# Spectral filter's channel mixing: from whole-array products, one unit at a time, to 64-row tiles of TensorE, two units at once

## The chip, the cores and the metric

The kernel runs on one core of a Trainium2 chip. The metric is the device time of one execution in microseconds, median of several runs. In the profile PE is TensorE's matmul, PEld its weight load, DVE is VectorE, ACT ScalarE, POOL GpSimd, and SPq the queue from which most DMAs are issued. All times are microseconds unless marked ns.

## What is computed

Two layers work on x, (2, 128, 128, 128) in fp32: two images of 128 by 128 tokens with 128 channels. Each layer (weights left out of the signature):

```python
def layer(x):
    residual = x
    h = afno_filter(layer_norm(x, n1_g, n1_b), w1, b1, w2, b2)   # + its own input
    h = h + residual
    residual = h
    h = gelu(layer_norm(h, n2_g, n2_b) @ mw1 + mb1)               # 128 -> 512
    return h @ mw2 + mb2 + residual                               # 512 -> 128

def afno_filter(x, w1, b1, w2, b2):                               # channels in 8 blocks of 16
    xf = rfft2(x, axes=(1, 2), norm='ortho')                      # 128 x 65 frequencies
    xr, xi = real(xf), imag(xf)                                   # einsum: block-diagonal 16 x 16
    o1r = relu(xr @ w1[0] - xi @ w1[1] + b1[0])
    o1i = relu(xi @ w1[0] + xr @ w1[1] + b1[1])
    o2r = softshrink(o1r @ w2[0] - o1i @ w2[1] + b2[0], 0.01)
    o2i = softshrink(o1i @ w2[0] + o1r @ w2[1] + b2[1], 0.01)
    return irfft2(o2r + 1j * o2i, s=(H, W), axes=(1, 2), norm='ortho') + x
```

## The kernel before

The program is a list of four steps, two layers by two images (`STEPS`), and in each step PE's queue is written as `dft_w`, `filter_`, `idft_h`, `mlp`. The engines' queues are written out by hand and meet in counting semaphores; nothing reorders them.

`dft_w` transforms along the width: 32 groups of four channels, each a 128x512 PSUM bank, evicted by ACT and DVE (`evict_a`) into the spectra, whose layout is (column frequency, channel half, real or imaginary, 64 channels of the half).

`filter_` is the stage that the change touches. Its work is cut into 34 units (`UNITS`): a unit n is four column frequencies (`GROUP`) of one channel half, q = n % 2; units 0 and 1 hold frequencies 0 to 3, units 2 and 3 ("alone") the Nyquist column only, the rest four frequencies each. Per unit:

- PE `dft_h` (L562): transform along the height, four fp32 products of 128 columns into bank q (0 or 1). A product's 128 output rows are 64 channels real and 64 channels imaginary.
- ACT `g_copy` (L826) copies that bank to `gsb`; for the first two units it also copies the Nyquist rows to `nyq` (L829).
- PE `mix1` (L573): the first complex mixing with the block-diagonal `w1s` as stationary operand, 128 by 128; the even part (L583, 65 of each 128 columns) and the odd part (L585, 63) use different weights. Output in bank 2 + q.
- ACT `e_copy` (L834) copies the even part to `usb`; DVE `combine` (L1089, two instructions, L1095 and L1096) adds and subtracts the odd part from PSUM; ACT `o_relu` (L840) adds the bias and takes the relu into `osb`.
- PE `mix2` (L606): four products with the data `osb` as stationary operand (128 by 128) and `w2s` as the moving one (128 columns), output transposed, in bank 4 + q.
- DVE `shrink` (L1099): bias (L1105, out of PSUM into `vsb`), clamp (L1107), difference (L1120, into the arena for the inverse transform).

The order around it: PE's loop in `filter_` (L616) is mix1 of unit n + 1, dft_h of a later unit (four ahead in the count), mix2 of unit n. `mix1` of a unit waits until `combine` of the unit two before it (the same bank) is done (`u_out`), `mix2` waits for `o_relu` (`o_out`) and for L1105 of the unit two before it (`v_out`). DVE's loop `batch` (L1266) is combine of the next unit, shrink of this one. `edges` mixes frequency 0 and Nyquist together once a step (PE L643, DVE L1122 and `edges_out` L1136). In the first step PE ends the filter with `keep_warm` products, in the later ones with `fc1_held`, the MLP products of a tile held back from the step before. `idft_h` begins when all but the last shrink are done.

The weights are built from packed blocks: DMAs into `wraw`, `vectors`, `b2rep` (on ACT's queue for layer 0, L886 to L893, on SP's for layer 1, `load_spectral` L391), multiplied by masks on POOL (`build_spectral`), scaled on DVE (`scale_spectral`) after a small product on PE (`dc_bias`).

The fences of rows further down name these lines; an fp32 product of the source appears in them as two loads and two matmuls.

## Time and profile before

| | us |
|---|---|
| median of 3 runs (lowest, highest) | 1652.82 (1651.64, 1653.29) |
| the profiled execution, its time | 1653.2 |
| the profiled execution, its span | 1651.4 |
| PE busy in the span | 1598.6 (97%) |
| PEld busy | 1445.4 (88%) |
| DVE busy | 1076.1 (65%) |
| ACT busy | 938.4 (57%) |
| POOL busy | 619.8 (38%) |

The granted TensorE clock is at its full level in all slices of the span. In the page, a group's row gives the line, engine, operation, output and input with their shapes, how many there were, busy time and mean duration. In a timeline a row gives the start, the length of the merged group, engine, line and operation; matmuls are pipelined, so the time that one takes up on PE is the distance of starts and not its own duration. A shape such as 64*128 64x65 is 64 rows by 128 columns of weights, with 65 moving columns.

### The profile page before, as it was taken

Reading aid. Unit: us, or ns where it says so; the run is one execution under the profiler, and the core shown is the slowest. Engines: PE = TensorE matmul, PEld = TensorE weight load, DVE = VectorE, ACT = ScalarE, POOL = GpSimd, SP = SyncE. Lnnn points to the kernel's source line nnn. Section 1 sums busy time; section 2 is a strip of 40 time slices with the busy share of each in tenths; the row PEclk is TensorE's granted clock in tenths of the full one; section 3 lists DMA queues with packets and bytes.
Section 4 is the critical chain, followed back from the end, with each engine's and each line's share of the span. In section 5 each row is a group of like instructions: output and inputs, shape, how many; then the busy total and the mean of one; then the engine's idle time right before and its main releaser. Section 6 shows DMA issues by size and latency. Waiting matters only on the chain.

```text
span 1651.4 us, 34968 instructions
## 1 busy us (share of the span) xinstructions
PE 1598.6 (97%) x11278; PEld 1445.4 (88%) x11278; DVE 1076.1 (65%) x2697; ACT 938.4 (57%) x1782; POOL 619.8 (38%) x774
## 2 busy tenths in 40 slices
PE   0999999999999999999999999999999999999999
PEld 0999988888999988888899998888889998888888
DVE  7889566556559856655656966665664995555453
ACT  5655276666535546666644545666663553666665
POOL 4800046766800016676660002677673000211111
PEclk9999999999999999999999999999999999999999
DMA  7500713333300062333320042333331006011111
GB/s 222 197 15 1 238 45 108 95 102 121 97 14 1 8 236 83 108 95 102 122 78 1 1 166 94 101 108 101 102 110 46 1 1 204 27 32 38 32 39 45
DMA packets 167249, 137.67 MB, mean 83 GB/s; under 512 B 9459, under 2 KB 131189, under 8 KB 167157
## 3 DMA queue, kind: packets, MB, share of 16 engines
q1 hardware_dynamic: 166354, 136.23, 26.1%
q8 instruction: 59, 0.97, 0.3%
q10 hardware_dynamic: 802, 0.21, 0.1%
q14 instruction: 34, 0.27, 0.1%
HBM read 69.29 MB, written 67.11 MB: 83 GB/s over the span
## 4 chain that ended last, share of the span: by engine, by line
PE 79%; DVE 14%; issue 4%; ACT 1%; SPq 1%; DVEq 1%; DMA 1%; POOL 0%; ACTq 0%
PE ps L756 27%; PE ps L558 7%; PE ps L722 7%; PE ps L724 7%; PE ps L683 7%; PE ps L723 7%; DVE vsb L1105 4%; PE ps L716 3%; PE ps L702 3%; PE ps L708 3%; DVE csb L1107 3%; DVE usb L1095 3%; DVE usb L1096 2%; PE ps L568 2%; PE ps L612 2%
## 5 line engine op out<-in xcount | busy, mean ns | idle before, releaser
L756 PEld LDWEIGHTS ps<-mw,gel 128*128 128x128 f32 x4000 | 520.6, 191 | 42.3
L756 PE MATMUL ps<-mw,gel 128*128 128x128 f32 x4000 | 523.7, 274 | 0.0
L875 ACT ACTIVATE gel<-ps,mb1f 128x512 f32<-128x512 f32 x500 | 343.7, 687 | 250.5 <-PE ps L724 219.7
L1460 POOL TENSOR_TENSOR arena<-arena,mb2rep 128x512 f32<-128x512 f32 x125 | 160.1, 1281 | 654.6 <-ACT hn L861 654.6
L722 PE MATMUL ps<-hth,mw1h 128*128 128x512 f32 x512 | 260.3, 508 | 2.9 <-DVE htl L1206 1.5
L1449 POOL TENSOR_SCALAR arena<-xnext,rstd,shift 128x128 f32<-128x128 f32 x360 | 159.3, 462 | 207.6 <-DVE shift L1344 207.6
L861 ACT ACTIVATE hn<-arena,shift,rstd 128x128 f32 (+1 forms) x512 | 221.7, 483 | 16.7 <-DVE shift L1344 16.7
L1189 DVE TENSOR_TENSOR arena<-ps,arena 128x512 f32 (+1 forms) x60 | 41.5, 691 | 252.4 <-PE ps L708 233.8
L724 PE MATMUL ps<-hth,mw1l 128*128 128x512 f32 x512 | 202.1, 395 | 0.0
L723 PE MATMUL ps<-htl,mw1h 128*128 128x512 f32 x512 | 200.8, 392 | 0.0
L846 ACT ACTIVATE osb<-usb,vectors 128x512 f32<-128x512 f32 (+1 forms) x136 | 95.6, 703 | 158.3 <-DVE usb L1096 158.3
L1206 DVE TENSOR_TENSOR htl<-ps,hth 128x512 fp32r<-128x512 f32 x128 | 88.2, 689 | 97.3 <-ACT hth L869 97.3
L612 PE MATMUL ps<-w2s,osb 128*128 128x128 f32 x1040 | 140.4, 277 | 2.3 <-ACT osb L846 2.3
L568 PEld LDWEIGHTS ps<-cst,arena 128*128 128x128 f32 x1024 | 132.9, 191 | 6.5 <-issue 0.8
L568 PE MATMUL ps<-cst,arena 128*128 128x128 f32 x1024 | 135.9, 276 | 0.3
L612 PEld LDWEIGHTS ps<-w2s,osb 128*128 128x128 f32 x1040 | 126.9, 192 | 6.9 <-ACT osb L846 6.3
L1407 POOL TENSOR_TENSOR gz<-arena,gain 128x512 f32<-128x512 f32 x96 | 123.7, 1290 | 7.0
L558 PE MATMUL ps<-cst,arena 128*128 128x128 f32 x1024 | 121.4, 282 | 1.0 <-POOL arena L1420 1.0
L558 PEld LDWEIGHTS ps<-cst,arena 128*128 128x128 f32 x1024 | 120.9, 196 | 1.1 <-DVE arena L1063 1.1
L869 ACT CAST hth<-ps 128x512 fp32r<-128x512 f32 x128 | 75.2, 587 | 80.1 <-PE ps L716 80.1
L683 PEld LDWEIGHTS ps<-cst,arena 128*128 128x128 f32 x1024 | 115.3, 192 | 1.3
L683 PE MATMUL ps<-cst,arena 128*128 128x128 f32 x1024 | 116.1, 275 | 0.0
(118 smaller groups left out, 2397.9 us busy)
## 6 DMA issues: line engine op xcount, KB each, us to landing
arena<-aside SPq DMA_DIRECT2D x128, 256.0 KB, 5.0
aside<-gz SPq DMA_DIRECT2D x96, 256.0 KB, 3.0
between<-xout SPq DMA_DIRECT2D x62, 256.0 KB, 2.3
out_dram<-xout SPq DMA_DIRECT2D x62, 256.0 KB, 2.3
xnext<-between SPq DMA_DIRECT2D x60, 256.0 KB, 3.1
aside<-first SPq DMA_DIRECT2D x32, 256.0 KB, 2.3
xnext<-in_x_dram SPq DMA_DIRECT2D x30, 256.0 KB, 3.1
first<-in_x_dram SPq DMA_DIRECT2D x1, 960.0 KB, 7.2
```

The source lines that it names most:

```text
L558: mm = pe.matmul(ps[:, 2 + cg % 4, P * i:P * i + P], rows_of(s)[:, (GROUP * cg + i) // 2, :, i % 2], FW, start=True, stop=True)
L568: mm = pe.matmul(ps[:, q, P * i:P * i + P], spec_of(s)[:, GROUP * b + i, q].rearrange("p r c -> p (r c)"), FH, start=True, stop=True)
L612: mm = pe.matmul(ps[:, 4 + q, P * i:P * i + P], osb[:, q, i, :], w2s[:, q].rearrange("p r c -> p (r c)"), start=True, stop=True)
L683: mm = pe.matmul(ps[:, cg % 4, P * i:P * i + P], y_of(s)[:, q, ch, :], IH, start=True, stop=True)
L722: pe.matmul(bank, h, hth[:, r % 2, :], start=True, stop=False)
L723: pe.matmul(bank, h, htl[:, r % 2, :], start=False, stop=False)
L724: pe.matmul(bank, l, hth[:, r % 2, :], start=False, stop=True).then_inc(f1_mm, 1)
L756: mm = pe.matmul(ps[:, r % 2, P * i:P * i + P], gel[:, r % 2, m, P * i:P * i + P], mw2[:, s // IMAGES, m, :], start=(m == 0 and i == 0), s ...
L861: ins = act.activation(hn[:, r % 2, i, :], row, ACT.Identity, bias=shift[:, r // 2, r % 2 * ROWS + i:r % 2 * ROWS + i + 1], scale=rstd[:, ...
L875: act.activation(gel[:, r % 2, m, :], ps[:, 2 + m % 2], ACT.Gelu, bias=mb1f[:, s // IMAGES, m:m + 1]).then_inc(gelu_out, 1)
L1449: ins = pool.tensor_scalar(zrow(s + 1, h0 + k), pairs(xnext[:, r, k, :]), rstd[:, r // 2, row:row + 1], shift[:, r // 2, row:row + 1], ALU ...
L1460: pool.tensor_tensor(t, t, b, ALU.add).then_inc(mb2_done, 1)
```

## The change

The channels of each half q are laid out anew in the spectra. Before, the 128 rows of a unit were (64 real, 64 imaginary); after, they are (g, real or imaginary, 32 channels), with g a half of the channel half. As the mixing is block-diagonal in blocks of 16 channels, no product crosses g, so a 128 by 128 weight matrix becomes two of 64 by 64, on rows 0 to 63 and 64 to 127. For q = 1 the two g change places between rows of the input and rows of the output.

- `mix1` now takes a pair p of units (n = 2p and 2p + 1) and issues, for the even and the odd part, four products of 64 rows and 64 output rows: (q, g) on rows 64 g, output rows 64 (g ^ q). It waits for both `gsb` copies and for `combine` of both units of the pair before; the semaphore rises by two at the last product.
- `mix2` takes the pair as well: for q, frequency and g a product with 64 rows of `osb` (128 columns) as stationary operand and 64 columns of `w2s`, output in banks 4 to 7, alternating by pair; again one rise at the end.
- PE's order is mix1 of pair p + 1, mix2 of pair p, both dft_h of pair p + 2. DVE's is combine of a unit of the next pair, shrink of a unit of this pair, for q = 0, 1. ACT's is both e_copy, o_relu, both g_copy, o_relu.
- The Nyquist unit reads `gsb` directly (32 rows deep), so `nyq` and its copies are gone.
- `edges` comes after mix2 of pair 4, and pair 5 waits for `edges_out`; `keep_warm` and `fc1_held` move behind the last mix2.
- `w1s`, `w2s` and the masks are half as wide; the blocks are loaded in 13 pieces with `b2rep` (`load_weights`), and the vectors in five (`load_vectors`), on SP's queue behind the constants in layer 0. The loops over evictions of the spectra are split in two by g.

The diff, cut to its core:

```diff
-            def mix1(s, n):
-                g, q = spectrum_of(n), n % 2
-                alone = n in (2, 3)
+            def mix1(s, p):
+                alone = p == 1
                 if not alone:
-                    pe.wait_ge(g_out, 2 * BATCHES * s + g + 1)
-                if n >= 2:
-                    pe.wait_ge(u_out, UNITS * s + n - 1)
...
+                    pe.wait_ge(g_out, 2 * BATCHES * s + spectrum_of(2 * p + 1) + 1)
+                if p:
+                    pe.wait_ge(u_out, UNITS * s + 2 * p)
+                def quarters(j0, j1, depth, k0, k1, kind, start):
+                    for q in range(2):
+                        for g in range(2):
+                            own_rows = slice(HALF * g + depth[0], HALF * g + depth[1])
+                            cols = slice(HALF * (g ^ q), HALF * (g ^ q) + HALF)
...
+                            mm = pe.matmul(dst[:, :, k0:k1], w1s[own_rows, kind, q].rearrange("p r c -> p (r c)"),
+                                           gsb[own_rows, q, j0:j1, k0:k1], start=start, stop=True, skip_group_check=True)
+                    return mm
...
+                elif p:
+                    quarters(0, GROUP, (0, HALF), 0, EVEN, 0, True)
+                    mm = quarters(0, GROUP, (0, HALF), EVEN, P, 1, False)
...
-                mm.then_inc(m1_mm, 1)
+                mm.then_inc(m1_mm, 2)
-            def mix2(s, n):
-                q, kws = n % 2, 1 if n in (2, 3) else GROUP
-                pe.wait_ge(o_out, UNITS * s + n + 1)
-                if n >= 2:
-                    pe.wait_ge(v_out, UNITS * s + n - 1)
-                for i in range(kws):
-                    mm = pe.matmul(ps[:, 4 + q, P * i:P * i + P], osb[:, q, i, :],
-                                   w2s[:, q].rearrange("p r c -> p (r c)"), start=True, stop=True)
-                mm.then_inc(m2_mm, 1)
+            def mix2(s, p):
+                kws = 1 if p == 1 else GROUP
+                if p >= 2:
+                    pe.wait_ge(v_out, UNITS * s + 2 * p - 2)
+                for q in range(2):
+                    pe.wait_ge(o_out, UNITS * s + 2 * p + q + 1)
+                    for i in range(kws):
+                        for g in range(2):
+                            own_rows = slice(HALF * g, HALF * (g + 1))
+                            at_ = 2 * HALF * 2 * q + HALF * i
+                            mm = pe.matmul(ps[:, 4 + 2 * (p % 2) + g, at_:at_ + HALF], osb[own_rows, q, i, :],
+                                           w2s[own_rows, q].rearrange("p r c -> p (r c)"), start=True, stop=True)
+                mm.then_inc(m2_mm, 2)
...
+                for p in range(PAIRED):
+                    if p + 1 < PAIRED:
+                        mix1(s, p + 1)
+                    if p == EDGE_PAIR + 1:
+                        pe.wait_ge(y_done, (UNITS + 1) * s + 2 * EDGE_PAIR + 2)
+                    mix2(s, p)
+                    if p == EDGE_PAIR:
                         edges(s)
+                    if p and p + 2 < PAIRED:
+                        for q in range(2):
+                            dft_h(s, 2 * p + 4 + q)
+                if s:
+                    fc1_held(s, 0)
+                    fc1_held(s, 1)
+                else:
+                    pe.wait_ge(v_out, UNITS * s + UNITS - 2)
+                    keep_warm(8, 6)
...
-                    g_copy(s, n + 1, 1)
-                    e_copy(s, n, 0)
+                    for q in range(2):
+                        e_copy(s, n + q, q)
                     o_relu(s, n, 0)
                     if not last:
-                        g_copy(s, n + 2, 0)
-                    e_copy(s, n + 1, 1)
+                        for q in range(2):
+                            g_copy(s, n + 2 + q, q)
                     o_relu(s, n + 1, 1)
...
+                def batch(b, odd, last=False):
                     for q in range(2):
-                        if not (last and q):
-                            combine(s, 2 * b + 3 + q, 1 - q)
-                        shrink(s, 2 * b + 2 + q, b, q)
...
+                        if not last:
+                            combine(s, 2 * b + 4 + q, q)
+                        shrink(s, 2 * b + 2 + q, b, q, odd)
```

## Rows read from the trace of the kernel before

**Rows 1.** The page: span, and busy time of the engines.

```profile
span 1651.4 us, 34968 instructions
...
PE 1598.6 (97%) x11278; PEld 1445.4 (88%) x11278; DVE 1076.1 (65%) x2697; ACT 938.4 (57%) x1782; POOL 619.8 (38%) x774
```

**Rows 2.** The page: chain that ended last, its shares by engine.

```profile
PE 79%; DVE 14%; issue 4%; ACT 1%; SPq 1%; DVEq 1%; DMA 1%; POOL 0%; ACTq 0%
```

**Rows 3.** Busy time in a window of the filter of step 1, with its header.

```profile
core 0: us, PE busy (x) PEld busy (x) DVE busy (x) ACT busy (x) POOL busy (x), PEclk, DMA share, GB/s
520.00:552.00 32.00, 32.00 (x243) 30.66 (x241) 29.76 (x61) 17.91 (x37) 0.00 (x0) 1.00 0.00 1
```

**Rows 4.** Timeline, one unit (start, length, engine, line, operation, shapes).

```profile
519.76 0.60 PE L583 MATMUL ps<-gsb,w1s 128*128 128x260 f32 x2
519.96 0.69 DVE L1105 TENSOR_TENSOR vsb<-ps,b2cols 128x512 f32<-128x512 f32 x1
...
520.20 0.59 PE L585 MATMUL ps<-gsb,w1s 128*128 128x252 f32 x2
...
520.62 1.05 PE L568 MATMUL ps<-cst,arena 128*128 128x128 f32 x8
...
521.51 1.06 PE L612 MATMUL ps<-w2s,osb 128*128 128x128 f32 x8
521.86 0.41 DVE L1095 TENSOR_TENSOR usb<-usb,ps 128x252 f32<-128x252 f32 x1
522.19 0.41 DVE L1096 TENSOR_TENSOR usb<-usb,ps 128x252 f32<-128x252 f32 x1
...
522.41 0.60 PE L583 MATMUL ps<-gsb,w1s 128*128 128x260 f32 x2
522.61 0.69 DVE L1105 TENSOR_TENSOR vsb<-ps,b2cols 128x512 f32<-128x512 f32 x1
```

**Rows 5.** Timeline, the end of the same filter.

```profile
564.92 0.68 DVE L1105 TENSOR_TENSOR vsb<-ps,b2cols 128x512 f32<-128x512 f32 x1
...
567.47 0.68 DVE L1105 TENSOR_TENSOR vsb<-ps,b2cols 128x512 f32<-128x512 f32 x1
...
569.39 2.83 PE L683 MATMUL ps<-cst,arena 128*128 128x128 f32 x23
```

**Rows 6.** Timeline, the start of the same filter.

```profile
478.82 0.57 PE L583 MATMUL ps<-gsb,w1s 128*128 128x195 f32 x2
478.98 0.26 ACT L829 COPY nyq<-ps 64x128 f32<-64x128 f32 x1 [0.31 <-PE ps L568]
...
479.22 0.48 PE L585 MATMUL ps<-gsb,w1s 128*128 128x189 f32 x2
...
479.63 0.43 PE L583 MATMUL ps<-gsb,w1s 64*128 64x65 f32 x2
...
479.91 0.38 PE L585 MATMUL ps<-gsb,w1s 64*128 64x63 f32 x2
480.22 0.30 PEld L602 LDWEIGHTS ps<-vectors,cst 128*128 128x128 f32 x2
480.22 0.38 PE L602 MATMUL ps<-vectors,cst 128*128 128x1 f32 x2
...
484.19 0.69 DVE L1105 TENSOR_TENSOR vsb<-ps,b2cols 128x512 f32<-128x512 f32 x1 [0.59 <-PE ps L612]
...
493.08 0.68 DVE L1105 TENSOR_TENSOR vsb<-ps,b2cols 128x512 f32<-128x512 f32 x1
```

**Rows 7.** Timeline, step 0's MLP bias: weight loads for one moving column.

```profile
201.55 0.97 PEld L693 LDWEIGHTS ps<-columns,mw1raw 128*128 128x128 f32 x8
```

**Rows 8.** Timeline, SP's issues at the layer's change.

```profile
571.91 0.55 SPq L393 DMA_DIRECT2D wraw<-in_L_blocks_dram  x1
```

**Rows 9.** The page: the matmuls of idft_h, all four steps.

```profile
L683 PE MATMUL ps<-cst,arena 128*128 128x128 f32 x1024 | 116.1, 275 | 0.0
```

More of the change, by code:

```diff
@@ L181, in afno @@
         paired = [a.rearrange("p (t h e) -> p t h e", h=H, e=2) for a in flat]
[L182 removed]
+        spectra = [a.rearrange("p (k a g b d) -> p k a g b d", a=2, g=2, b=2, d=QUART) for a in flat]
         columns_of = [a.rearrange("p (q c k) -> p q c k", q=2, c=HALF) for a in flat]
@@ L235, in afno @@
         csb = at("csb", [P, 2, HALF, GROUP, 2], o); o += size(csb.shape)
-        nyq = at("nyq", [P, 2, P], o); o += size(nyq.shape)
         yedge = at("yedge", [P, 2, 2, HALF, 2], o); o += size(yedge.shape)
@@ L588, in mix1 @@
-                even, odd = (w1s[:, i, q].rearrange("p r c -> p (r c)") for i in range(2))
-                if alone:
-                    dst = ps[:, 2 + q, 0:P].rearrange("p (j k) -> p j k", j=1)
-                    mm = both(dst, nyq[HALF:P, q].rearrange("p (j k) -> p j k", j=1), odd[HALF:P], even[HALF:P], True)
-                else:
-                    dst = ps[:, 2 + q].rearrange("p (j k) -> p j k", j=GROUP)
-                    src = gsb[:, q]
-                    if g >= 2:
-                        mm = both(dst, src, even, odd, True)
-                    else:
-                        both(dst[:, 1:], src[:, 1:], even, odd, True)
-                        both(dst[:, 0:1], src[0:HALF, 0:1], even[0:HALF], odd[0:HALF], False)
+                    pe.wait_ge(g_out, 2 * BATCHES * s + spectrum_of(2 * p + 1) + 1)
@@ L625, in filter_ @@
                 mix1(s, 0)
[L626 to L641 removed]
+                for q in range(2):
+                    dft_h(s, 4 + q)
+                for p in range(PAIRED):
[5 more added lines that the diff above has]
+                    if p == EDGE_PAIR:
+                        edges(s)
+                    if p and p + 2 < PAIRED:
[7 more added lines that the diff above has]
+                    keep_warm(8, 6)
             def edges(s):
                 pe.wait_ge(t_edge, s + 1)
+                pe.wait_ge(v_out, UNITS * s + 2 * EDGE_PAIR)
                 for i, m in enumerate((REVERSE, IDENT)):
@@ L836, in e_copy @@
                 act.wait_ge(m1_mm, UNITS * s + n + 1)
+                if not (isinstance(n, int) and n < 2):
+                    act.wait_ge(o_out, UNITS * s + n - 1)
                 src = ps[:, 2 + q].rearrange("p (j k) -> p j k", j=GROUP)
@@ L907, in _ @@
                 for q in range(2):
-                    with act.Fori(0, CGROUPS // 8) as j:
-                        for r in ((0, 2) if s else range(4)):
-                            a_out(s, q, j, r)
+                    for g in range(2):
+                        with act.Fori(0, CGROUPS // 16) as j:
+                            for r in ((0, 2) if s else range(4)):
+                                a_out(s, q, g, j, r)
                 if s:
@@ L919, in _ @@
                     e_copy(s, q, q)
+                for q in range(2):
                     o_relu(s, q, q, first=True)
@@ L1249, in _ @@
                     for q in range(2):
-                        with dve.Fori(0, CGROUPS // 8) as j:
-                            for r in (1, 3):
-                                a_out(s, q, j, r)
+                        for g in range(2):
+                            with dve.Fori(0, CGROUPS // 16) as j:
+                                for r in (1, 3):
+                                    a_out(s, q, g, j, r)
                         if q == 0 and s % IMAGES == 0:
```

178 lines of the change are left out of this document (93 added, 85 removed).

## The prediction

> **What bounds the kernel now.** Read the shares of the engines first [rows 1]: PE is busy for 1598.6 of 1651.4 us, DVE for 1076.1. The chain of work that ended last gives PE 79% and DVE 14% [rows 2]. So the kernel as a whole is PE's. But a share over the whole span does not say what the changed stage is worth, and the change touches one stage, the filter, which runs once in each of four steps. So read a window of its steady part: in 32 us PE is busy for 32.00, DVE for 29.76 and ACT for 17.91 [rows 3]. Both PE and DVE are close to full there, and only the timeline tells them apart.
>
> One unit of the filter takes 2.65 us: vsb (L1105) starts at 519.96 and again at 522.61 [rows 4]. PE's issue in it: even half of mix1 0.44, odd half 0.42, dft_h 0.89, mix2 0.90 (differences of starts in rows 4), 2.65 together, so PE has no gap. DVE: shrink from L1105 to L1095 takes 1.90 and combine from L1095 to the end of L1096 0.74, but L1105 of the next unit begins right behind the last mix2 matmul's end (521.51 + 1.06 = 522.57). Where PE is not the one that is late, at the filter's end, DVE goes from L1105 to L1105 in 2.55 [rows 5]. So PE binds by 2.65, and DVE stands 0.10 behind it. That is the first reading: per pair of units 5.30 now, and 5.10 as the floor that DVE sets even if mixing cost PE nothing. From the fifth unit to the last but one (493.08 to 567.47, 14 pairs) the filter takes 74.4 [rows 5, 6].
>
> **The change, what it gives PE to do.** Each fp32 product is two loads and two matmuls, one after the other (x2 in every group of rows 4). What a matmul costs is its columns: (0.44 / 2) = 0.22 for 260 columns, 0.21 for 252, 0.11 for 128.
>
> First mixing (M1, both units of a pair). Before: 4 products, 8 matmuls, 2 x 0.44 + 2 x 0.42 = 1.72. After: 2 kinds x 4 tiles = 8 products of the same 260 or 252 columns, 16 matmuls. The trace has no two tiles in it, so M1 is bounded: if all four tiles run at once, 2 x 0.22 + 2 x 0.21 = 0.86; if none do, 3.44. I take what lies between, for this reason: a product's second matmul needs the same tile as its first and starts behind it, and matmuls start in order (every pair in rows 4 does), so a new tile's first matmul can only run beside the old tile's second. That makes 9 slots of 0.215: 1.94. Twice the matmuls, two at a time: nothing is gained.
>
> Second mixing (M2, both units). Before: 8 products, 16 matmuls, 1.78. After: 16 products with 64 moving columns in place of 128, 32 matmuls, but each still loads 128 columns (osb is the stationary side). What a load costs is seen where the matmul is tiny: eight loads with one moving column each take 0.97 and two take 0.30, so (0.97 - 0.30) / 6 = 0.111 each [rows 6, 7], the same as with 128 moving columns. Loads of 64 rows are no cheaper: the two pairs with 64-row weights and 63 to 65 columns start 0.28 apart, 0.14 a matmul [rows 6]. So the halved columns buy nothing. If the two row tiles load side by side, by the same slots, 17 x 0.111 = 1.89 (at best 16 x 0.111 = 1.78); if loads queue, 32 x 0.111 = 3.55. Only if a load were not the limit would it be 0.9. I take 1.89.
>
> The Trainium skill speaks against this part too: "TensorE: Matmul & The Clock Gate", section LDWEIGHTS, says a load's time goes by its columns and not by its rows, 128 / 1.2 = 107 ns here as an estimate; the trace's 111 ns agrees, and by it M2 cannot be half of what it was.
>
> Change of tile shape. Where the 64-row matmuls follow full ones the step is 479.63 - 479.22 = 0.41 for two matmuls of 189 columns (0.32 by columns), and back again 0.31 for two that need 0.22 [rows 6]: 0.09 each way. A pair now has three such changes, two of them (into M1, into M2) on the path below: 0.2. Nothing (a change costs none) to 0.3 are its bounds.
>
> **What it does to the order.** Before, unit n+1 was mixed while unit n was combined, in the other PSUM bank. Now a pair takes both banks, and the waits close a ring: mix1 of pair p+1 waits for combine of both units of pair p (u_out); PE then does M1, and M2 of pair p behind it; only the end of M2 releases shrink of its first unit; DVE's queue holds combine of the second unit of pair p+1 behind that shrink; and that combine releases mix1 of p+2. No dft_h lies in the ring, it runs beside DVE (1.78, under 2.64), and so do the copies on ACT. The ring is
>
> L = M1 + M2 + shapes 0.2 + handovers 0.25 + shrink 1.90 + combine 0.74.
>
> Handovers: the last matmul's tail 1.06 - 8 x 0.111 = 0.17, and 0.04 to DVE [rows 4], the same 0.04 back. L = 1.94 + 1.89 + 0.2 + 0.25 + 2.64 = 6.92 against 5.31 on average now. PE's own sum, 1.94 + 1.89 + 1.78 + 0.3 = 5.9, is shorter: after the change neither engine is full, the ring binds. Over 14 pairs: 14 x 6.92 = 96.9, against 74.4: +22.5 a step.
>
> The start of the filter. mix1 of the first pair waits for both gsb copies instead of one (+0.8), takes about 2.4 for both units, then both combines, then mix1 of the short pair, then M2 before the first shrink: adding the same pieces I get the first L1105 2.9 later (484.19 now), and the fifth unit's about 6 later (493.08 now) [rows 6], since two more M1 and an M2 stand in line. +22.5 + 6 = 28.5 a step, x 4 = +114.
>
> **Edits with one answer.** The nyq copies go (0.26 each on ACT [rows 6], under PE's work). More and smaller weight loads: at the start ACT issues them in front of its first activation, with later waits of DVE's statistics that take it up; at the layer's change SP issues 12 more in front of xnext and the residual loads, at 0.55 each 7 us [rows 8], beneath 29 us of idft_h (116.1 / 4, [rows 9]): nothing, and as a bound 2 once, if the first residual tiles come late. Eviction of the spectra, gsb, usb and the sums of DVE keep their element counts: 0. shrink reads two banks instead of one, with the same 512 elements: 0, and bounds of 0.1 either way a pair. fc1_held moves behind the last mix2, where PE waits for DVE anyway (idft_h starts 1.92 after the last but one L1105, in both) [rows 5].
>
> Sum: 1653.2 (the profiled run's time, span 1651.4, beside a median of 1652.8) + 114 = 1767.
>
> **The rivals.**
> - All tiles at once: M1 0.86, M2 1.78, L = 5.73. Start +2.8. (14 x 5.73 - 74.4 + 2.8) x 4 = +34: 1687; with shapes at nothing 1674. For it: the four tiles share neither cells nor partitions of one bank. Against: the order of starts above. The Trainium skill has this rule ("TensorEngine Tiling (Array Packing)", Key Properties: tiles load and multiply in parallel; a change of mode drains); no row here shows it, and even with it the ring keeps the time above today's.
> - Faster than before: the load is not what 0.111 stands for, M2 is 0.9. Then L = 4.85, under DVE's 5.10, DVE binds, and 14 x 5.10 - 74.4 = -3.0, start +1: -2 a step, 1645. It decides at M1 + M2 below 2.2. For it: rows of full tiles only say what full tiles do. Against: rows 7, and 64-row loads in rows 6.
> - Loads of row tiles queue: M2 3.55. With M1 1.94, L = 8.58, start +9.3: +220, 1873. With M1 0.86, L = 7.5: +147, 1800.
> - It does not do what it says, tiles run one after another: M1 3.44, M2 3.55, L = 10.1, start +12: +318, 1970.
>
> **How the numbers follow.** Forecast case 0.36, all at once 0.20, loads queue 0.20 (0.13 with the slots, 0.07 without), one after another 0.10, faster 0.10, and 0.04 for a mix that ends within 0.2% (what a measurement can tell from no change here). Time 1767. The range leaves out the faster case and the serial one: 1673 to 1875. Faster 0.10, same 0.04, slower 0.86.
>
> **What would show it.** In a steady pair of the profile after: 64-row mix1 matmuls x16 from first start to last within 1.9 (0.9: all at once; 3.4: none); mix2 x32 within 1.9 (0.9, 1.8 or 3.5 likewise); L1105 of the first unit idle before it with PE as releaser, about 1.8 a pair; PE busy share of the window under 90% while dft_h still takes 0.89 a unit; L1105 to L1105 over a pair 6.9. A period of 5.1 with DVE gapless would make me wrong on the load; the granted clock below 1.00 in the window would be a cause I have not counted.

## The result, and the profile after

The changed kernel takes 1711.86 us (median of 4 runs, 1710.35 to 1716.47), beside 1653.05 for the kernel before on the same chip: a ratio of 1.0362, 95% interval [1.0341, 1.0382]. It is slower by 59 us. The forecast was 1767, the range 1673 to 1875. The sign and the range hold, but the forecast's own case does not: the pair of units takes 5.86 us and not 6.92, near the 5.73 of the rival in which all tiles run at once. And a cause that no term of the sum had, the granted clock, carries about a third of the 63 us lost in the profiled execution.

The page of the changed kernel: span, the engines' busy time, the chain, and from the list of costliest groups the lines of the two mixings (busy and mean, then the idle time just before and what ended most of it).

```profile
span 1714.7 us, 38110 instructions
...
PE 1597.6 (93%) x12900; PEld 1414.2 (82%) x12900; DVE 1072.8 (63%) x2697; ACT 953.3 (56%) x1774; POOL 616.4 (36%) x774
...
PE 87%; DVE 7%; issue 2%; ACT 2%; SPq 1%; DMA 1%; DVEq 0%; POOL 0%; ACTq 0%
...
L645 PE MATMUL ps<-w2s,osb 64*128 64x64 f32 x2080 | 142.0, 289 | 7.4 <-ACT osb L883 7.4
...
L614 PE MATMUL ps<-gsb,w1s 64*64 64x252 f32 (+5 forms) x1152 | 77.2, 384 | 58.2 <-DVE usb L1129 43.9
...
L1140 DVE TENSOR_TENSOR vsb<-ps,b2cols 128x512 f32<-128x512 f32 (+1 forms) x136 | 90.2, 663 | 50.3 <-PE ps L645 50.3
```

Beside the page of before [rows 1, 2], PE has the same busy time in a longer span, 93% in place of 97%. Two idle times are new: 58.2 us of PE ahead of the first mixing, mostly ended by DVE's combine (L1129), and 50.3 of DVE ahead of the shrink (L1140), ended by PE's second mixing. Each engine waits for the other: that is the ring of the prediction.

Over a steady stretch (520 to 552 us) PE is busy for 27.15 of 32 us at the full clock, where before it was busy for all 32 [rows 3].

One pair in the timeline (start, length, engine, line, operation, shapes; in brackets the idle time before it and its releaser):

```profile
542.32 1.86 PEld L593 LDWEIGHTS ps<-cst,arena 128*128 128x128 f32 x16
542.33 2.05 PE L593 MATMUL ps<-cst,arena 128*128 128x128 f32 x16
542.44 0.69 DVE L1140 TENSOR_TENSOR vsb<-ps,b2cols 128x512 f32<-128x512 f32 x1 [0.67 <-PE ps L645]
...
544.67 0.41 DVE L1129 TENSOR_TENSOR usb<-usb,ps 128x252 f32<-128x252 f32 x1
545.00 0.68 DVE L1140 TENSOR_TENSOR vsb<-ps,b2cols 128x512 f32<-128x512 f32 x1
...
545.23 1.09 PE L614 MATMUL ps<-gsb,w1s 64*64 64x260 f32 x16 [0.85 <-DVE usb L1129]
...
546.25 1.86 PEld L645 LDWEIGHTS ps<-w2s,osb 64*128 64x128 f32 x32 [0.38 <-issue]
546.26 2.00 PE L645 MATMUL ps<-w2s,osb 64*128 64x64 f32 x32
...
548.30 0.69 DVE L1140 TENSOR_TENSOR vsb<-ps,b2cols 128x512 f32<-128x512 f32 x1 [0.67 <-PE ps L645]
```

Follow the ring from shrink to shrink: shrink of unit 0 and combine of unit 1, 542.44 to the end of L1129 at 545.08, 2.64; 0.15 to PE; the first mixing, M1, from 545.23 to 546.26, 1.03; the second, M2, to its end at 548.26, 2.00; 0.04 to DVE. Sum 5.86. The transforms L593 run beside the shrink, outside the ring, as foreseen.

How the first mixing runs shows in a slice of the same timeline, 545.20 to 545.35: the group holds only what overlaps the slice.

```profile
545.20 0.24 PEld L614 LDWEIGHTS ps<-gsb,w1s 64*64 64x64 f32 x8 [1.02 <-ACT gsb L867]
545.23 0.45 PE L614 MATMUL ps<-gsb,w1s 64*64 64x260 f32 x4 [0.85 <-DVE usb L1129]
```

Four matmuls start together. The single starts in the trace are 545.232, .239, .245 and .252, then four more from 545.475, from 545.694 and from 545.905: four waves of four, some 0.22 apart, the time of one matmul of 260 or 252 columns. The second mixing goes in 16 waves of two, every 0.11, but for the first wave, which stands 0.16 ahead of the second, and the last, which stands 0.20 ahead of the first transform.

What the timeline does not show at once is TensorE's clock. Two windows of the changed kernel, the start of the filter in steps 1 and 3, and the busy lines of PE there:

```profile
core 0: us, PE busy (x) PEld busy (x) DVE busy (x) ACT busy (x) POOL busy (x), PEclk, DMA share, GB/s
500.00:510.00 10.00, 6.92 (x50) 5.48 (x52) 7.95 (x23) 4.78 (x10) 0.00 (x0) 0.66 0.00 0
...
1325.00:1355.00 30.00, 26.04 (x202) 21.53 (x202) 17.70 (x44) 11.58 (x24) 0.00 (x0) 0.60 0.01 1
```
```profile
498.03 2.00 PE L645 MATMUL ps<-w2s,osb 64*128 64x64 f32 x32
502.44 1.99 PE L614 MATMUL ps<-gsb,w1s 64*64 64x260 f32 x16 [2.41 <-DVE usb L1129]
```

After an idle time of 2.41 us the same 16 matmuls take 1.99 in place of 1.09, at the lower of the clock's two levels (1.2 GHz of 2.4), called half clock in what follows. The trace's record of the clock has such a stretch of 6.8 us some 11 us behind the first dft_h of steps 0 to 2 and of 23.9 us in step 3, and one of 6.8 us at each filter's end. Before, the record has none ahead of the last 4 us of the run.

In one account, from the first dft_h of a step (before and after, steps 1 and 3):

| mark | before, every step | after, step 1 | after, step 3 |
|---|---|---|---|
| first shrink | +7.54 | +9.21 | +9.21 |
| fifth shrink | +16.43 | +21.79 | +23.94 |
| last but one shrink | +90.82 | +103.83 | +111.27 |
| first idft_h | +92.74 | +106.42 | +113.88 |

Step 1 loses 13.7: 5.35 at the start, 7.65 over 14 pairs (5.86 against 5.31), 0.66 at the end. That the mean of the 14 is the 5.86 of a steady pair is chance: the steady pairs take 5.86 (before 5.30), one that has the edges in it 6.55, and the last one 5.36, of which the half clock at the end is some 0.9 (the same pair takes 4.50 in e7_warm below, where the clock holds). The four steps lose 14.5, 13.7, 14.0 and 21.1, 63.3 together, which is the whole difference of the profiled runs (1716.47 against 1653.2 us). Nothing is lost outside the filter.

### The profile page after: what moved, and what is told of

It is laid out like the page before. It is cut to its first block, busy times and chain, and to the rows that moved or that the text cites. A ratio compares the mean times of both kernels' runs of the same rounds, so it can differ in the third digit from the quotient of the medians.

```text
span 1714.7 us, 38110 instructions
## 1 busy us (share of the span) xinstructions
PE 1597.6 (93%) x12900; PEld 1414.2 (82%) x12900; DVE 1072.8 (63%) x2697; ACT 953.3 (56%) x1774; POOL 616.4 (36%) x774
## 4 chain that ended last, share of the span: by engine, by line
PE 87%; DVE 7%; issue 2%; ACT 2%; SPq 1%; DMA 1%; DVEq 0%; POOL 0%; ACTq 0%
PE ps L793 26%; PE ps L645 8%; PE ps L583 7%; PE ps L759 7%; PE ps L761 7%; PE ps L760 7%; PE ps L720 7%; PE ps L614 5%; PE ps L593 3%; PE ps L753 3%; PE ps L739 3%; PE ps L745 3%; DVE vsb L1140 2%; DVE csb L1142 1%; DVE usb L1128 1%
## 5 line engine op out<-in xcount | busy, mean ns | idle before, releaser
L645 PEld LDWEIGHTS ps<-w2s,osb 64*128 64x128 f32 x2080 | 131.5, 200 | 33.5 <-issue 24.7
L645 PE MATMUL ps<-w2s,osb 64*128 64x64 f32 x2080 | 142.0, 289 | 7.4 <-ACT osb L883 7.4
L593 PE MATMUL ps<-cst,arena 128*128 128x128 f32 x1024 | 140.8, 294 | 0.3
L593 PEld LDWEIGHTS ps<-cst,arena 128*128 128x128 f32 x1024 | 128.9, 204 | 5.0 <-issue 0.8
L614 PE MATMUL ps<-gsb,w1s 64*64 64x252 f32 (+5 forms) x1152 | 77.2, 384 | 58.2 <-DVE usb L1129 43.9
L583 PE MATMUL ps<-cst,arena 128*128 128x128 f32 x1024 | 121.4, 282 | 1.4 <-POOL arena L1459 1.4
L583 PEld LDWEIGHTS ps<-cst,arena 128*128 128x128 f32 x1024 | 120.9, 196 | 1.6 <-DVE arena L1096 1.6
L1140 DVE TENSOR_TENSOR vsb<-ps,b2cols 128x512 f32<-128x512 f32 (+1 forms) x136 | 90.2, 663 | 50.3 <-PE ps L645 50.3
```

Of the source, the lines that this page charges most:

```text
L583: mm = pe.matmul(ps[:, 2 + cg % 4, P * i:P * i + P], rows_of(s)[:, (GROUP * cg + i) // 2, :, i % 2], FW, start=True, stop=True)
L593: mm = pe.matmul(ps[:, q, P * i:P * i + P], spec_of(s)[:, GROUP * b + i, q].rearrange("p g r c -> p (g r c)"), FH, start=True, stop=True)
L614: mm = pe.matmul(dst[:, :, k0:k1], w1s[own_rows, kind, q].rearrange("p r c -> p (r c)"), gsb[own_rows, q, j0:j1, k0:k1], start=start, stop ...
L645: mm = pe.matmul(ps[:, 4 + 2 * (p % 2) + g, at_:at_ + HALF], osb[own_rows, q, i, :], w2s[own_rows, q].rearrange("p r c -> p (r c)"), start ...
```

## The experiments

Three questions: what the tiles themselves cost or save, what closes the ring, and what the clock takes. The runs e2, e3, e4, e5 and e10 were executed once each, and how long they stood at half clock differs; so their pairs are what is compared, and their whole times only loosely.

**e4_same_tile: the order of the products.** The forecast of M1 rested on matmuls starting in order. Here both products of one tile stand behind each other, then those of the next tile.

```
-    quarters(0, GROUP, (0, HALF), 0, EVEN, 0, True)
-    mm = quarters(0, GROUP, (0, HALF), EVEN, P, 1, False)
+    for q in range(2):
+        for g in range(2):
+            for kind, k0, k1 in ((0, 0, EVEN), (1, EVEN, P)):
+                mm = pe.matmul(dst[:, :, k0:k1], w1s[own_rows, kind, q]..., gsb[own_rows, q, :, k0:k1], ...)
```

> The changed kernel with mix1's eight products ordered by tile (even and odd part of one tile one behind the other, then the next tile) instead of by part. Theory (each tile takes its matmuls as it comes free, whatever the order): 16 matmuls in four waves as now, mix1 1.03, pair 5.86. Rival (matmuls start in the order of the queue, so only neighbours on different tiles run together): 12 or 13 waves of 0.215, mix1 2.7, pair 7.5, about 1805.

PE in the timeline of e4_same_tile:

```profile
548.70 1.12 PE L629 MATMUL ps<-gsb,w1s 64*64 64x260 f32 x16 [0.86 <-DVE usb L1136]
549.75 2.00 PE L652 MATMUL ps<-w2s,osb 64*128 64x64 f32 x32
```

M1 is 1.05 (548.70 to 549.75), as good as with the tiles in turn. In the single starts the eight passes of the even products (260 columns) come first, four at 548.70 to .75 and four at 548.95 to 549.02, and then the eight of the odd ones (252), although the program has them alternating within each tile. So a tile's next matmul does not wait for matmuls that stand ahead of it in the queue for other tiles: the premise of the slots is refuted. The whole took 1727.24 us, with the pair at 5.89; most of what it is over the changed kernel is half clock, 89 us at it where the changed kernel's profile has 72, and 34.1 of them in step 0 alone.

**e3_move128 and e2_load64: what a second mixing of row tiles costs.** One doubles the moving columns (64 to 128, products that nobody needs), the other halves the loaded ones (128 to 64, so half of the second mixing's outputs are left out).

```
-    mm = pe.matmul(ps[:, ..., at_:at_ + HALF], osb[own_rows, q, i, :], w2s[own_rows, q]...)
+    mm = pe.matmul(ps[:, ..., at_:at_ + P], osb[own_rows, q, i, :], w2s[own_rows]...)             # e3
+    mm = pe.matmul(ps[HALF * g:HALF * g + HALF, ...], osb[own_rows, q, i, 0:HALF], w2s[own_rows, q]...)   # e2
```

> The changed kernel with 128 moving columns instead of 64 in each product of mix2, so that it computes what it doesn't need and overwrites outputs of its own. Theory (the load is the limit): nothing changes, mix2 1.93 and the pair 5.86, since a matmul of 128 columns takes the 0.111 that the load takes. Rival (the moving columns count): mix2 goes to 3.5 or so, the pair to 7.4.

> The changed kernel with mix2 loading 64 of osb's 128 columns in each of its 32 products (the other half of the outputs is left out; 16 products before the first step write the banks once). Theory (two row tiles load side by side and the load of 128 columns, 0.111, is the limit of mix2): 64 columns load in half the time, mix2 falls from 1.93 to about 1.0 and the pair from 5.86 to 5.10 (DVE) at least. Rival (the issue of 32 load and matmul pairs is the limit): mix2 stays at 1.9, the pair at 5.86.

PE in e3_move128, then PE and DVE in e2_load64:

```profile
542.78 2.06 PE L645 MATMUL ps<-w2s,osb 64*128 64x128 f32 x32
544.77 2.05 PE L593 MATMUL ps<-cst,arena 128*128 128x128 f32 x16
```
```profile
539.57 0.68 DVE L1143 TENSOR_TENSOR vsb<-ps,b2cols 128x512 f32<-128x512 f32 x1
...
542.35 1.09 PE L614 MATMUL ps<-gsb,w1s 64*64 64x260 f32 x16 [1.11 <-DVE usb L1132]
...
543.24 1.13 PE L645 MATMUL ps<-w2s,osb 64*64 64x64 f32 x32
...
544.67 0.68 DVE L1143 TENSOR_TENSOR vsb<-ps,b2cols 128x512 f32<-128x512 f32 x1
```

Twice the moving columns cost 0.06 (2.06 for 2.00; the pair 5.92 for 5.86). The whole took 1702.89 us, less than the changed kernel, with 27 us of it at half clock. Half the loaded columns take the second mixing to 1.13 and the pair to 5.10, where DVE goes without a gap (539.57 to 544.67), and the whole to 1648.91 us. These products are 64 by 64 like the first mixing's, so no change of shape lies between the two, and M1 gives way to M2 after 0.89 (542.35 to 543.24) in place of 1.03: that change costs 0.14. The loads are the second mixing's price, and DVE's floor of 5.10 is where the prediction put it.

**e5_mix2_full: row tiles against the whole array.** The changed kernel, but the second mixing as 8 whole products for a pair.

```
-    for g in range(2):
-        mm = pe.matmul(ps[:, 4 + 2 * (p % 2) + g, at_:at_ + HALF], osb[own_rows, q, i, :], w2s[own_rows, q]...)
+    mm = pe.matmul(ps[:, 4 + 2 * (p % 2) + q, P * i:P * i + P], osb[:, q, i, :], w2s[:, :]...)
```

> The changed kernel with the second mixing as one product of the whole array for each unit and column group, as before the change, instead of two row tiles; the first mixing stays in four tiles, pairs and signals stay where they are. (The weights of the second mixing are stand-ins of the right size, so the values are not the reference's; its time is what is read.) Theory A (what sets the second mixing's time is loading 128 columns for each product at 111 ns, in two row tiles side by side or in one whole array alike, so the row tiles buy nothing): the second mixing of a pair takes 16 x 0.111 = 1.78 us where the row tiles take 1.93, and a pair takes 5.86 - 0.15 = 5.71 us or a little under. Rival B (two row tiles of half the rows do save something that a whole-array product pays): the second mixing of a pair takes over 2.0 us and a pair 5.95 us or more.

```profile
545.02 1.09 PE L614 MATMUL ps<-gsb,w1s 64*64 64x260 f32 x16 [1.04 <-DVE usb L1126]
...
551.95 2.05 PE L642 MATMUL ps<-w2s,osb 128*128 128x128 f32 x16
```

The whole products take 2.05 where the row tiles take 2.00, and 1.89 against 1.93 to the first transform behind them; the pair takes 5.90 where it took 5.86. Neither 5.71 nor 5.95 came, but theory A's reason holds: row tiles buy next to nothing (0.05 at the end, and nothing at the start of what follows). Its 1.78 left out the change of shape and the last matmul's tail. The whole took 1697.30 us, with 20 us at half clock.

**e1_split: hand over each unit.** M2's unit 0 goes to banks of its own and signals its shrink at once, so half of M2 leaves the ring.

```
-    mm = pe.matmul(ps[:, 4 + 2 * (p % 2) + g, at_:at_ + HALF], ...)
-mm.then_inc(m2_mm, 2)                       # once a pair
+    mm = pe.matmul(ps[:, 4 + 2 * q + g, HALF * i:HALF * i + HALF], ...)
+    mm.then_inc(m2_mm, 1)                   # once a unit, with a wait on v_out for each unit
```

> The changed kernel, with mix2's output laid out by unit (banks 4 + 2q + g) and one rise of the semaphore per unit, so that shrink of a pair's first unit no longer waits for the second unit's products; edges moves behind mix1 of pair 6, into bank 4. Theory (a ring M1 + M2 + shrink + combine sets the pair's 5.86): half of M2, 0.96, leaves the ring, which gives 4.90; DVE's own 5.10 then binds, 14 x (5.10 - 5.86) x 4 = -43 against the changed kernel, some 1669, PE 4.83 of 5.10 busy. Rival (PE's queue, with its changes of tile shape, is what binds, and the ring only mirrors it): the pair stays at 5.7 to 5.9 and the time within 5 us of 1712.

```profile
540.26 2.00 PE L644 MATMUL ps<-w2s,osb 64*128 64x64 f32 x32
...
542.19 2.05 PE L593 MATMUL ps<-cst,arena 128*128 128x128 f32 x16
...
543.38 0.58 ACT L865 COPY gsb<-ps 128x512 f32<-128x512 f32 x1 [1.00 <-PE ps L593]
...
544.28 0.58 ACT L865 COPY gsb<-ps 128x512 f32<-128x512 f32 x1 [0.31 <-PE ps L593]
...
544.92 1.09 PE L614 MATMUL ps<-gsb,w1s 64*64 64x260 f32 x16 [0.68 <-ACT gsb L865]
```

1699.05 us, ratio 1.0295 [1.0267, 1.0324], and a pair of 5.68: a miss of the theory, which had 5.10 and 1669, and just outside the rival's 5.7 to 5.9 too. DVE no longer waits for PE, so the first ring was there and is gone, but a second ring stood right behind the first: M2 1.93, both transforms, the second copy of gsb (0.58, behind the last transform), M1 1.03. The change had put dft_h directly ahead of the mixing that reads it, and a pair's mixing needs both copies.

**e6_order and e8_act_order: take the queues apart.** Both build on e1_split. e6 issues dft_h ahead of the second mixing and does both combines ahead of both shrinks. e8 adds ScalarE's order.

```
     mix1(s, p + 1)
+    if p and p + 2 < PAIRED:
+        for q in range(2):
+            dft_h(s, 2 * p + 4 + q)
     mix2(s, p)
-    (the same three lines stood here)
...
-    combine(q=0); shrink(q=0); combine(q=1); shrink(q=1)
+    combine(q=0); combine(q=1); shrink(q=0); shrink(q=1)                      # e6, DVE
...
-    o_relu(s, n, 0); g_copy(s, n + 2, 0); g_copy(s, n + 3, 1); o_relu(s, n + 1, 1)
+    g_copy(s, n + 2, 0); g_copy(s, n + 3, 1); o_relu(s, n, 0); o_relu(s, n + 1, 1)   # e8, ACT
```

> The kernel of the split signal (e1_split) with two moves of order. PE issues the two transforms dft_h of the pair after next between the first mixing of the next pair and the second mixing of this pair, not behind it, so that their evictions are over before the first mixing that needs them is due; and VectorE does both combines of the next pair ahead of both shrinks of this pair, so that no combine waits for a second mixing. Theory A (both parts of PE's chain, the hand-over of a whole pair and the gsb copies behind dft_h, are gone; the tiles' gain on PE is then free to show, and VectorE is the next limit): a pair takes VectorE's 5.10 us (the period of e2_load64), 0.20 less than the 5.30 of the kernel before, 14 x 0.20 = 2.8 us less in a step; the start of the filter and its end keep some 0.9 + 1.5 us of what e1_split shows there, so 1650 us, 1645 to 1662 with what the clock takes at the start. Rival B (PE is the limit at 1.03 + 1.93 + 1.87 us and a hand-over at each of three changes of kind): 5.3 to 5.5 us for a pair, 1655 to 1675 us. Rival C (the order doesn't free the chain, a wait of another kind takes its place): 5.6 us or more for a pair, 1690 us or more.

> The kernel of e6_order with ScalarE's order changed too: the two gsb copies of the next pair stand ahead of both osb evictions of this one, where in e6_order they stood behind the first, which waited 2.33 us for a second mixing that PE had put behind the transforms. Theory A (that queue was what kept e6_order's pair at 5.96 us, and nothing else stands in the way): PE waits for nothing or next to nothing, a pair takes VectorE's 5.10 us or PE's own sum of 1.03 + 1.93 + 1.87 and three changes of kind, 5.0 to 5.2 us together; S4 to S32 of a step takes 71 to 73 us where before took 74.4, start and end keep 1 to 3 us over before, so 1645 to 1662 us. Rival B (a chain of another kind takes its place, as of the banks of the second mixing, which a unit's shrink frees): 5.4 us or more for a pair and 1670 us or more.

ACT and PE in e6_order, then PE in e8_act_order:

```profile
548.36 0.72 ACT L881 ACTIVATE osb<-usb,vectors 128x512 f32<-128x512 f32 x1 [2.33 <-PE ps L644]
548.99 1.05 ACT L865 COPY gsb<-ps 128x512 f32<-128x512 f32 x2
...
550.09 1.09 PE L614 MATMUL ps<-gsb,w1s 64*64 64x260 f32 x16 [0.95 <-ACT gsb L865]
```
```profile
536.61 1.09 PE L614 MATMUL ps<-gsb,w1s 64*64 64x260 f32 x16
...
537.63 2.05 PE L593 MATMUL ps<-cst,arena 128*128 128x128 f32 x16
...
539.62 2.00 PE L644 MATMUL ps<-w2s,osb 64*128 64x64 f32 x32
...
541.71 1.09 PE L614 MATMUL ps<-gsb,w1s 64*64 64x260 f32 x16
```

e6 was a miss, and its rival C came true: 1722.80 us, ratio 1.0426 [1.0405, 1.0447], a pair of 5.96, worse than e1_split. The copies of gsb still stood behind an osb eviction on ACT, and that eviction waited 2.33 us for a second mixing that now ran later. With ACT's order changed as well no engine waits for a queue: the pair is 5.10 (536.61 to 541.71), PE and DVE both nearly full (29.67 and 27.86 of 30 us), and the whole 1654.05 us, ratio 1.0009 [1.0000, 1.0018]. From the fifth shrink to the last but one a step takes 71.0 us where before took 74.4. This gain of 3.4 is used up at the filter's ends, below.

**e10_mix1_full: what the four tiles save.** e8 with the first mixing as whole products, two kinds for each unit.

```
-    quarters(0, GROUP, (0, HALF), 0, EVEN, 0, True)
-    mm = quarters(0, GROUP, (0, HALF), EVEN, P, 1, False)
+    mm = pe.matmul(dst[:, :, k0:k1], w1s[:, kind]..., gsb[:, q, :, k0:k1], ...)   # for q, for kind
```

> The kernel of e8_act_order with the first mixing of pairs 2 to 16 as products of the whole array, four for a pair (two units, two kinds), as before the change. (The weights are stand-ins of the right size, so the values are not the reference's; its time is what is read.) Theory A (the four tiles do halve the first mixing, and in the kernel of the change that gain was real on PE and lost in the chain): the first mixing of a pair takes 1.7 us in place of 1.03, PE becomes the limit and a pair takes 1.7 + 1.93 + 1.87 and up to 0.2 us, 5.5 to 5.75 us in place of 5.10, the whole 1675 to 1695 us. Rival B (the tiles save PE little, their four waves cost as much as the products of the whole array): a pair stays at 5.1 to 5.2 us and the time at 1652 to 1658 us.

```profile
541.41 2.00 PE L647 MATMUL ps<-w2s,osb 64*128 64x64 f32 x32
543.35 1.99 PE L626 MATMUL ps<-gsb,w1s 128*128 128x260 f32 x8
545.18 1.95 PE L593 MATMUL ps<-cst,arena 128*128 128x128 f32 x16
547.05 2.00 PE L647 MATMUL ps<-w2s,osb 64*128 64x64 f32 x32
```

The first mixing takes 1.83 (543.35 to 545.18) where the tiles take 1.02, PE has no gap, the pair is 5.64, and the whole 1684.29 us. So the tiles do what they say: 0.8 us of PE for a pair. In the changed kernel that gain was there and the ring took more than all of it.

**e7_warm: the clock.** The changed kernel with products that nothing reads in PE's idle stretches.

```
+    if p < 2 and s:
+        keep_warm((5, 10)[p], 7)
+    if p == PAIRED - 1:
+        keep_warm(4, 0)
     if p + 1 < PAIRED:
         mix1(s, p + 1)
```

> The changed kernel with products that nothing reads put into idle stretches of PE: in steps 1 to 3, 5 ahead of the first mixing of pair 1 and 10 ahead of that of pair 2 (where PE stood idle for 2.41 us), and in all steps 4 ahead of the second mixing of the last pair. Nothing else is moved. Theory A (TensorE's clock is granted at half after PE has idled, which is what stretched the first mixing of pair 2 to 1.99 us and the transforms behind it to 3.51): the half-clock stretches some 11 us behind the first dft_h are gone in steps 1 to 3 and still there in step 0; the fifth shrink comes 2 to 4 us earlier in these steps, and the whole is 1698 to 1706 us. Rival B (the clock falls for another cause, as the amount of work in the tiles): the stretches stay, and the time is that of the changed kernel, 1710 to 1716 us, or more by what the added products delay.

A window of e7_warm and the same mixing as above:

```profile
498.00:528.00 30.00, 27.70 (x337) 24.66 (x337) 18.07 (x47) 14.45 (x30) 0.00 (x0) 1.00 0.01 1
```
```profile
511.00 2.50 PE L805 MATMUL ps<-cst 128*128 128x128 f32 x20
513.49 1.09 PE L614 MATMUL ps<-gsb,w1s 64*64 64x260 f32 x16
```

1700.38 us, ratio 1.0282 [1.0266, 1.0298], 11 less than the changed kernel for added work. In the profiled execution (1709.55 us, the slowest of five), in steps 1 to 3 there is no half clock but 3.4 us at the end of step 3's filter, and the first idft_h comes at +103.15, +103.15 and +103.83, though the first shrink is 1.04 later than in the changed kernel. Step 0, left alone at its start as a control, had 34.1 us at half clock in this run and its first idft_h at +118.18. Theory A stands, and the median is inside its 1698 to 1706.

But an idle stretch does not settle how long the half clock lasts, or that it comes. Six profiles have this idle stretch of 2.4 us unfilled (the changed kernel, e2, e3, e4, e5, and step 0 of this run). There the clock fell inside it or within 1.6 us behind it in 18 of 21 steps; with it filled, in none of three. Up to where the clock falls, step 0 of this run has the program and the idle stretches of step 0 of the changed kernel (0.77 us at +2.2, 2.41 at +9.1), and 34.1 us at half clock where that has 6.8. And step 2 of e3_move128 has them too, with none at half clock before the filter's end, and the mixing behind the 2.41 us at its full speed:

```profile
911.36 1.09 PE L614 MATMUL ps<-gsb,w1s 64*64 64x260 f32 x16 [2.41 <-DVE usb L1129]
```

**e9_end, e11_end_warm, e12_end_warm7: the end of the filter.** In e8_act_order PE stood idle for 2.09 us ahead of the last second mixing, which then took 3.76 in place of 2.00:

```profile
562.71 3.76 PE L644 MATMUL ps<-w2s,osb 64*128 64x64 f32 x32 [2.09 <-ACT osb L881]
```

e9, on top of e8, moves the held products there; e11 and e12, on top of e9, fill what is left.

```
+    if p == PAIRED - 1:                     # ahead of the last mix2
+        keep_warm(3, 0)                     # e11, e12; s > 0
+        fc1_held(s, 0); fc1_held(s, 1)      # e9; step 0: keep_warm(11, 0)
...
+        keep_warm(5, 2)                     # e11, between its two units; e12: 3
...
+    keep_warm(14, 2)                        # e11, ahead of idft_h; e12: 7
```

> The kernel of e8_act_order with the end of the filter changed: PE does the two held products for fc1 (in step 0: 11 products that nothing reads) between the second mixing of pair 15 and that of the last pair, where it stood idle for 2.09 us, into banks 0 and 1, which the last transforms have left. Theory A (in e8_act_order the transforms idft_h start at +92.47 because the held products stand behind the last pair's second mixing, and that took 3.76 us instead of 2.00 at the half clock that followed PE's idling): the last second mixing takes 2.0 us, idft_h starts at +89 to +90.5 in steps 1 to 3, 2 to 3.5 us earlier in each step, and the whole is 1640 to 1648 us. Rival B (something other than PE's idling takes the clock, or the start of idft_h hangs on VectorE's shrinks of the last pair): idft_h at +92 or later, 1652 to 1656 us.

> The kernel of e9_end with products that nothing reads put into PE's three idle stretches at the filter's end (3 ahead of the held products, 5 between the two units of the last second mixing, 14 ahead of idft_h). e9_end starts idft_h 1.9 us earlier in a step than the kernel before and is no faster, and its granted clock is 0.72 in the 11 us behind that start where the kernel before has 1.00. Theory A (the half clock that follows PE's idling of 0.50, 0.68 and 1.87 us takes that gain back): the half-clock stretches behind the start of idft_h are gone, idft_h starts at +91 or earlier, and the whole is 1643 to 1649 us, faster than both kernels. Rival B (the clock falls for another cause, as the tiles' work in the filter, or the gain is lost in idft_h or behind it even at full clock): 1651 to 1656 us.

> The kernel of e11_end_warm with fewer of the products that nothing reads: 7 in place of 14 ahead of idft_h, 3 in place of 5 between the two units of the last second mixing. In e11_end_warm the half clock behind the start of idft_h was gone, but each such product is two records and the 14 took 3.39 us, so idft_h started 1.9 us later than the shrinks allowed. Theory A (both halves of the end are now right: full clock, and idft_h at +90.9 to +91.2 in steps 1 to 3, where e11_end_warm has +92.8): the gain of the filter, 1.6 to 1.9 us in a step, reaches the end of the step: 1644 to 1648 us, faster than both kernels. Rival B (the gain is met again behind idft_h, by a transfer or by VectorE, whose times of arrival don't move): idft_h at +91 and the next step's first dft_h still at +398.5 or later, 1650 to 1653 us.

The 11 us from 566 on, behind the start of idft_h, in e9_end and in e12_end_warm7, and PE ahead of idft_h in e11_end_warm and in e12_end_warm7:

```profile
566.00:577.00 11.00, 11.00 (x72) 11.00 (x73) 4.16 (x7) 2.34 (x4) 0.15 (x1) 0.72 0.13 26
```
```profile
566.00:577.00 11.00, 11.00 (x100) 10.93 (x99) 5.97 (x10) 2.93 (x5) 0.00 (x0) 1.00 0.12 22
```
```profile
567.11 3.39 PE L804 MATMUL ps<-cst 128*128 128x128 f32 x28
570.34 3.85 PE L724 MATMUL ps<-cst,arena 128*128 128x128 f32 x33
```
```profile
565.46 1.83 PE L804 MATMUL ps<-cst 128*128 128x128 f32 x14
567.20 6.04 PE L724 MATMUL ps<-cst,arena 128*128 128x128 f32 x52
```

e9_end took its last second mixing at full clock and started idft_h at +90.85, 1.9 ahead of the kernel before, and was no faster: 1653.71 us, ratio 1.0005 [0.9996, 1.0014], because idft_h then ran 6.8 us at half clock (72 matmuls in the window, 100 in e12). Neither theory had that. e11 kept the clock but gave the time away: its 14 products are 28 matmuls of 3.39 us, idft_h at +92.8, 1652.59 us, ratio 1.0004 [0.9995, 1.0013]. With half of them both are right: idft_h at +90.85, the next step's first dft_h at +396.84 (before +398.76), and 1645.09 us (1644.59 to 1647.13), ratio 0.9958 [0.9944, 0.9971]. This beats both kernels, the one before by 7 us.

## Why the prediction was right and where it was wrong

- **The ring** is right: which waits close it, that dft_h and the copies stay outside, that neither engine is full (PE 85% of a steady stretch, under the 90% forecast). Its sum in measured terms is 5.86, and it stays above the 5.31 of before. DVE's wait for PE is 0.67 a pair, where 1.8 was forecast.
- **M1** is the step that failed. Forecast 1.94, "nothing is gained"; measured 1.03. The nine slots rested on matmuls starting in the order of issue, which every pair of rows 4 does; but these all use the whole array. Such rows had nothing to say on tiles, and the prediction took their order for a rule. e4_same_tile refutes it. The Trainium skill's page "TensorEngine Tiling (Array Packing)", Key Properties, was weighed for this and says that tiles load and multiply in parallel; the trace agrees, with four starts inside 0.02 us. The bound of 0.86 lacked only the change of shape. At 0.9 us a pair, 14 pairs and four steps this term alone put 51 us too much into the forecast.
- **M2** is right in size: forecast 1.89, measured 1.93 to the first transform behind it. It is right that loads carry it (e2, e3, e5) and that the two row tiles load side by side. The 17 slots are not: the starts come in 16 waves, the "at best" of 1.78, and 0.15 of change of shape makes up the size. The same premise failed here as in M1, and only its price is small. The Trainium skill's page "TensorEngine Tiling (Array Packing)", Theoretical Speedup, gives up to 2x where one dimension is at most 64; for M2, whose moving side went from 128 to 64, the runs show 2.00 against 2.05.
- **Shapes and handovers**: forecast 0.2 (at most 0.3) and 0.25. Measured: 1.03 - 0.86 in M1 and 1.93 - 1.78 in M2, 0.32; and 0.07 of tail, 0.15 to PE and 0.04 to DVE, 0.26. The 0.26 meets the forecast by offset, since that had 0.17 of tail and 0.04 to PE. With 2.64 for shrink and combine, as forecast, the sum closes: 0.86 + 1.78 + 0.32 + 0.26 + 2.64 = 5.86. These are the terms of the rival with all tiles at once, but for 0.12 of shapes.
- **The start of the filter**: forecast +6 at the fifth shrink, measured +5.35, and yet not right. The first shrink came 1.67 later, not 2.9. The tiles ran at once, for which the rival had +2.8, and the clock put the rest on. e7_warm, where the clock holds, has +3.6, in which the added products put the first shrink 1.04 later.
- **The end**: forecast 0, measured +0.66 in step 1 and +1.2 in step 0. PE idled for 0.97 and 0.54 us ahead of the two halves of the last second mixing, and the clock fell again. Some 0.9 more of that is in the last of the 14 pairs.
- **The clock** was named as an uncounted cause and not counted, though the prediction itself had PE idle for 1.0 of a pair's 6.92 (its sum for PE was 5.9). The steps of e7_warm without half clock lose 10.4 each to the kernel before, 41.6 for four; the changed kernel loses 63.3. So the clock takes some 22 us of it in that run, and a little more without the fillers' delay. It also varies from run to run: the changed kernel's runs spread over 6 us where before has 2, and the slowest has the lowest mean granted clock (0.979, the others 0.982 or 0.983).
- **Edits at nothing** were nothing: the time outside the filter did not move.
- **Faster than before** decided at M1 + M2 below 2.2. They came to 2.96, and in e2_load64, where they are 1.94, the pair is 5.10 as worked out and the time 1648.91.

With the tiles of M1 at once (0.86), all other terms of L left as they were and the start at +2.8, the prediction's sum is (14 x 5.84 - 74.4 + 2.8) x 4 = +41: about what the steps at full clock lose in e7_warm, 41.6. Term by term it is less close, 7.4 over the pairs against 6.8 and 2.8 at the start against 3.6. The rest, up to the +63 of the profiled run, is the clock's. So the measured time lies as near to the forecast as it does partly by luck: the range holds because it takes in nearly every way of being slower, M1 was 0.9 a pair too dear, and the clock, which was not counted, gave some 22 us of that back.

Two sums of the rivals are a little off, and nothing hangs on them: with shapes at nothing (14 x 5.53 - 74.4 + 2.8) x 4 is +23, so 1676 and not 1674, and with tiles one after another (14 x 10.1 - 74.4 + 12) x 4 is +316 and not +318.

What stays open is what decides whether the clock falls after an idle stretch and for how long: after the same 2.4 us it did not fall in three steps, and stood at half for 3.4, 6.8, 13.7, 23.9 or 34.1 us in the others.

## What to carry to other kernels

When work is joined into larger pieces, its hand-overs grow with it: list for each engine what stands queued behind every wait, because here three of them in turn (the whole pair's signal, the copies behind the transforms, ScalarE's eviction) each kept the pair above the 5.30 of before (5.86, 5.68, 5.96), and repairing two of the three was slower than repairing one. Tiles of the array paid where moving columns were the price, and row tiles did not where the loads were. Before counting a new idle time of PE as harmless or an earlier start as a gain, look at the granted clock behind it: the same reordering was worth nothing at half clock and 7 us at full.

## What the runs showed of the hardware

- Four 64x64 tiles run at once for fp32 products: 16 matmuls of 260 and 252 columns in 1.03 us, where whole-array products of the same columns for the same output take 1.83. Their starts don't follow the order of issue across tiles (e4_same_tile: all products of 260 columns started before any of 252, though the two alternated in the program).
- Two row tiles of 64x128 load side by side: 32 loads of 128 columns in 1.86 us, as 16 of the whole array. With loads of 64 columns 32 matmuls take 1.13 (e2_load64). Moving 128 columns in place of 64 costs 0.06 us for all 32 (e3_move128).
- Going from 64x64 tiles to 64x128 ones costs 0.14 us: 1.03 from the start of M1 to that of M2, and 0.89 where M2 is of 64x64 tiles too (e2_load64).
- The granted clock fell to half at short idle times of PE: 0.50, 0.68 and 1.87 us stand close together at the filter's end in e9_end, its 6.8 us at half clock begin in the last of them, and filling them took it away (e12_end_warm7). It is not certain: at 2.4 us it fell in 18 of 21 steps, and with 0.85 us idle in each steady pair of 5.86 it stayed full.
- One product of 128 by 128 in fp32 that nothing reads costs two matmuls, 0.24 us together at full clock (14 of them 3.39), so it fills an idle stretch finely, and overfills it as easily.
